# Between the stages of a vision layer with routed experts: tails, first weights and shared pieces in another order

## The reference

```python
    h = _L0_tok_ref(x, L0_tok_W, ...)
    h = h + _L0_attn_ref(_layernorm(h, axis=-1), L0_attn_W_c)
    h = h + _L0_ffn_ref(_layernorm(h, axis=-1), ...)
```

```python
        h = layer_norm(x, ln_in_g, ln_in_b)
        gate = jax.nn.softmax((h @ router_w + router_b) / TEMP, axis=-1)
        vals, idx = jax.lax.top_k(gate, TOP_K)
        ...
        eh = jax.nn.silu(jnp.einsum('bsd,edh->ebsh', h, ew1) + eb1[:, None, None, :])
        ey = jnp.einsum('ebsh,ehd->ebsd', eh, ew2) + eb2[:, None, None, :]
        mix = jnp.einsum('bse,ebsd->bsd', comb, ey)
        shared = (jax.nn.silu(h @ sw1 + sb1) @ sw2 + sb2) * SHARED_SCALE
        moe_out = mix + shared
        fh = layer_norm(moe_out, ff_ln_g, ff_ln_b)
        ff_out = jax.nn.silu(fh @ ff_w1 + ff_b1) @ ff_w2 + ff_b2
        return x + moe_out + ff_out
```

## Time and profile before

| | us |
|---|---|
| median of three runs | 976.31 |
| the three runs | 982.05, 968.53, 976.31 |
| span of the profiled execution | 972.0 |

### The profile page before, as it was taken

The page is one execution under the profiler, slowest core; times in us unless marked ns, Lnnn a source line. Parts: engine busy times, 40 slices in busy tenths (PEclk is TensorE's granted clock), DMA queues, the critical chain, the costliest instruction groups (busy, mean ns, idle before and its releaser), DMA issues. The chain is left out here.

```text
span 972.0 us, 22164 instructions
## 1 busy us (share of the span) xinstructions
PE 896.2 (92%) x5920; PEld 801.2 (82%) x5920; DVE 676.2 (70%) x2244; ACT 599.5 (62%) x1064; POOL 438.8 (45%) x374
## 2 busy tenths in 40 slices
PE   2999999989999999999889999999999899789999
PEld 2788888778878888888779889898999899679888
DVE  8377877757877887787556666666676675488884
ACT  3567666656666666777645565555555565477766
POOL 6012554425555545554451445455555464334342
PEclk9999999979999999999879999999999999989999
DMA  9999999977788888767137687777778675334432
GB/s 225 224 221 225 242 247 240 237 205 210 213 228 218 214 216 219 194 216 213 50 105 215 196 227 218 214 219 228 216 224 236 184 221 166 107 82 115 107 103 57
DMA packets 194299, 186.96 MB, mean 192 GB/s; under 512 B 16797, under 2 KB 168698, under 8 KB 194010
## 3 DMA queue, kind: packets, MB, share of 16 engines
q1 hardware_dynamic: 183168, 166.24, 65.2%
q0 software_dynamic: 9376, 19.42, 6.1%
q10 hardware_dynamic: 1722, 0.93, 0.5%
HBM read 150.48 MB, written 36.04 MB: 192 GB/s over the span
## 5 line engine op out<-in xcount | busy, mean ns | idle before, releaser
L1435 PE MATMUL bank<-xf,wp 128*128 128x256 f32 x1280 | 314.0, 394 | 8.4 <-ACT xf L632 5.4
L1435 PEld LDWEIGHTS bank<-xf,wp 128*128 128x128 f32 x1280 | 237.7, 192 | 51.6 <-issue 7.4
L916 POOL DMA_INDIRECT y_tok<-region,dsti x160 | 162.9, 1018 | 164.9 <-DVE region L1268 119.0
L874 POOL TENSOR_TENSOR rstd<-var,neghalf 128x4 f32<-128x4 f32 (+2 forms) x51 | 80.6, 1580 | 287.9 <-DVE var L1030 156.4
L632 ACT ACTIVATE xf<-region 128x1024 f32<-128x1024 f32 x160 | 174.0, 1137 | 18.3 <-DVE region L947 18.3
L890 POOL DMA_INDIRECT z_rows<-z,posg x130 | 157.3, 1210 | 52.5 <-issue 52.2
L798 ACT ACTIVATE region<-bank,cols 128x256 f32<-128x256 f32 x320 | 132.3, 476 | 55.2 <-PE bank L1626 37.2
L1637 PE MATMUL bank<-region 128*128 128x128 f32 x1280 | 156.8, 275 | 1.1 <-DVE region L1268 1.0
L1637 PEld LDWEIGHTS bank<-region 128*128 128x128 f32 x1280 | 150.4, 192 | 1.7 <-issue 1.5
L1626 PE MATMUL bank<-parts 128*128 128x256 f32 x960 | 136.6, 290 | 14.2 <-DVE parts L1279 8.8
L1626 PEld LDWEIGHTS bank<-parts 128*128 128x128 f32 x960 | 119.6, 190 | 25.7 <-issue 19.0
(11 more groups left out here) (183 smaller groups left out, 1232.3 us busy)
## 6 DMA issues: line engine op xcount, KB each, us to landing
region<-in_x SPq DMA_DIRECT2D x384, 196.0 KB
region<-in_L_ffn_ew SPq DMA_DIRECT2D x160, 256.0 KB
region<-z_rows SPq DMA_DIRECT2D x80, 130.0 KB
region<-y_tok SPq DMA_DIRECT2D x16, 512.0 KB, 3.6
ht_dram<-hT SPq DMA_DIRECT2D x16, 256.0 KB
r_dram<-rr SPq DMA_DIRECT2D x16, 256.0 KB
region<-ht_dram SPq DMA_DIRECT2D x16, 256.0 KB, 5.5
region<-r_dram SPq DMA_DIRECT2D x16, 256.0 KB
```

Of the source, the lines that this page charges most:

```text
L874: pool.tensor_tensor(dst, var, neghalf[:, 0:var.shape[1]], ALU.pow).then_inc(ready, 1)
L916: pool.indirect_dma_start(y_tok, bass.IndirectOffsetOnAxis(dsti[n % 2][:, i:i + 1], 0), yout[n % 2][:, i], None).then_inc(y_free[n % 2], 16)
L1435: ins = pe.matmul(out_cols, wp[:, s], cols_in, start=s == 0, stop=s == MAIN - 1)
```

## The change

Four parts:

- SP zeroes the tails 4 to 11 before it waits for the scatters, not after it has loaded the rows of the tiles 0 to 3.
- SP loads w1 of tile 4 before its loops, and within them w1 of tile j + 1 between the rows and w2 of tile j. `four_loads` replaces the four calls of `expert_loads`; it loads the expert number of its first tile once more. The last four tiles are written out behind the second loop, which has one pass less.
- Pieces of the shared expert change places: on TensorE `sh_up(7)` goes ahead of the last group's transposes, and three pieces go ahead of the table's transposes; on ScalarE and VectorE the matching steps move with them.
- VectorE splits w1 of tile 0 before it waits for the table's transposes.

```diff
-            def expert_weights(j, n):
-                ex = sp.value_load(ejc[0:1, bass.ds(j, 1)], min_val=0, max_val=E - 1)
+            def expert(j):
+                return sp.value_load(ejc[0:1, bass.ds(j, 1)], min_val=0, max_val=E - 1)
+
+            def first_weight(j, n, ex):
                 sp.wait_ge(w1l_ready, j - 3)
                 sp.dma_start(w1b[n % 4], ew1[bass.ds(ex, 1)].rearrange("o d h -> d (o h)")).then_inc(w1_loaded[n % 4], 16)
+
+            def second_weight(j, n, ex):
                 sp.wait_ge(down_done, j - 3)
...
-            def expert_loads(j, n):
-
-                expert_rows(j, n)
-                expert_weights(j, n)
-
+            def four_loads(j, n, end=4):
+
+                ex = expert(j)
+                for m in range(4):
+                    expert_rows(j + m, n + m)
+                    if m < end:
+                        coming = expert(j + (m + 1))
+                        first_weight(j + (m + 1), n + m + 1, coming)
+                    second_weight(j + m, n + m, ex)
+                    ex = coming
+
+            zero_tails(sp, FIRST, SP_TAILS)
             sp.wait_ge(tails_first, 16 * FIRST)
             sp.wait_ge(z_free[0], 16 + 16 * TOPK + 16 * TOPK * GT * GROUPS // 2)
             sp.wait_ge(z_free[1], 16 + 16 * TOPK * GT * GROUPS // 2)
             for j in range(FIRST):
                 sp.dma_start(zin[j], z_rows[j * CAP:j * CAP + EROWS].rearrange("(p h) d -> p h d", p=P))\
                   .then_inc(zin_loaded[j], 16)
-            zero_tails(sp, FIRST, SP_TAILS)
+            sp.wait_ge(w1l_ready, 1)
+            sp.dma_start(w1b[0], ew1[FIRST]).then_inc(w1_loaded[0], 16)
...
-                for n in range(4):
-                    expert_loads(i * 4 + n, 4 + n)
+                four_loads(i * 4, 4)
             sp.dma_start(r_res[:, PATCH_TILES * D:], r_dram[:, PATCH_TILES]).then_inc(r_loaded, 16)
-            with sp.Fori(1 + GROUPS, EXPERT_TILES // 4) as i:
-                for n in range(4):
-                    expert_loads(i * 4 + n, 4 + n)
+            with sp.Fori(1 + GROUPS, EXPERT_TILES // 4 - 1) as i:
+                four_loads(i * 4, 4)
+            four_loads(EXPERT_TILES - 4, EXPERT_TILES - 4, end=3)
...
+            sh_silu(FILL)
             one(take_z, GROUPS)
-            shared(FILL)
+            ht_high(FILL + 2)
...
                 if not attn:
                     ht_low(FILL)
+                    sh_rows(4)
...
                 if not attn:
-                    sh_rows(4)
                     ht_low(FILL + 1)
+                    sh_rows(5)
...
             dve.tensor_copy(tail[:, :], base[0:1, :]).then_inc(tail_ready, 1)
+            ht_low(FILL + 2)
+            sh_rows(FILL - 1)
...
-            sh_rows(FILL - 2)
+            ht_low(FILL + 3)
+            split_w1(0, 0, 0)
             dve.wait_ge(tej_done, 1)
...
+            sh_up(FILL)
             t_zz(GROUPS, 0)
-            sh_up(FILL)
             gates(GROUPS, 0)
```

More of the change, by code:

```diff
@@ L1250, in _ @@
             dve.wait_ge(tab_ready, 1)
-            split_w1(0, 0, 0)
-            for i in range(FILL, EARLY):
+            sh_rows(FILL)
+            for i in range(FILL + 2, EARLY):
                 if i + 2 < EARLY:
@@ L1596, in _ @@
             sh_up(FILL + 1)
+            sh_down(FILL)
+            sh_up(FILL + 2)
+            sh_down(FILL + 1)
             pe.wait_ge(ejt_ready, 1)
@@ L1602, in _ @@
             pe.matmul(bank[7][:, 0:DYN], ones[:, :], ejd[:, :], start=True, stop=True).then_inc(ejb_done, 1)
-            for i in range(FILL + 2, EARLY):
-                sh_down(i - 2)
+            for i in range(FILL + 3, EARLY):
                 sh_up(i)
-            sh_down(EARLY - 2)
+                sh_down(i - 1)
             sh_down(EARLY - 1)
```

## The result

The changed kernel takes 996.73 us (median of six runs, 990.79 to 999.93) against 975.58 for the kernel before (six runs, 968.53 to 982.05): a ratio of 1.0219, 95% interval 1.018 to 1.0258. It is slower by 2.2%, 21 us, where I forecast 6 us slower. The sign was right; the time lies 0.7 us outside the range that I gave.

A forecast was written before the change was run, and what follows sets the result against it. SP, issuing without a pause, was taken to bound the second stage. Earlier start -6.0, extra load in seventeen passes +13.6 and end -1.4 gave +6.2 us on the median 976.31, put at 982; range 966 to 996.

The forecast's parts named there:

- SP sets the second stage: Expert tiles: SP, issuing without a pause, takes 15.68 us a pass where the PE alone needs 13.72.
- What would show it: List of signs for right or wrong, such as SP hardly waiting, a pass of 16.3 to 16.7 us, zin waits grown.
- The stretch of 15.68 over the clean 14.1: Expert loop: measured pass over one of four clean tiles plus 1.5 us; raised a load's price from 0.74 to 0.8 us.
- Asking for w1 a tile ahead removes none of SP's work: Expert loop: the earlier request leaves SP's work as it was; only the extra expert-number load was charged, 0.8 us a pass.
- Term (c): Expert loop until tile 76: seventeen passes with one more register load each, +13.6 us.
- Tails, 6.98 us hidden: Before the expert loop: eight tails on SP move inside its 8.3 us wait for the scatters, taking 6.98 us off.
- Shared pieces, -1.1 and -2.63 on the PE: Before the first expert tile: moved pieces bring the gates 1.1 us earlier and fill 2.63 us of PE idling.
- waits that were there: Before the expert loop: moved pieces on VectorE and ScalarE fall into existing waits, with no cost counted.
- the forecast 6 us earlier start of tile 8: Start of the expert loop: SP's zin load of tile 8 comes at 534.6 instead of 540.66, 6.0 us earlier.
- Term (d): Behind tile 76, where only the PE runs on: 20.2 us instead of 21.55 with w1 early, 1.4 us off.
- The whole stage speeds up: Rival, expert loop: SP's slow steps come from VectorE's lateness and vanish; -21.7 us, or 955; chance 0.06.
- hidden load: Rival, expert loop: the extra load disappears in waits the profile doesn't name; -8.2 us, or 968; chance 0.22.

The follow-up runs named there:

- e9: The kernel before, with SP's register loads stripped of the test of their bounds: ratio 1.0108 (1.0017 to 1.0199).
- e10: The kernel before, with a tile's row and expert numbers loaded together from one table, without the bounds test: ratio 1.0005 (0.997 to 1.004).
- e5: The kernel before, with GpSimd storing results to plain consecutive rows by direct DMAs instead of scatters: ratio 0.9695 (0.9582 to 0.9809).
- e6: The changed kernel, with GpSimd storing results to plain consecutive rows by direct DMAs instead of scatters: ratio 0.9682 (0.9558 to 0.9806).
- e4: The kernel before, with w1 asked for a tile ahead only inside a pass, still four expert numbers loaded: ratio 1.0162 (1.0106 to 1.0218).
- e14: The changed kernel, with GpSimd's second scatter of a tile held until the PE's second product of the next tile: ratio 1.0119 (1.0041 to 1.0197).
- e3: The kernel before, with one unused register load of an expert number added to each pass: ratio 1.0118 (1.0034 to 1.0202).
- e1: The changed kernel with the loop of before, leaving the moved shared pieces and tails: ratio 0.999 (0.9945 to 1.0034).
- e12: The changed kernel with the loop of before and the tails in their old place, leaving the moved pieces: ratio 0.999 (0.9954 to 1.0027).
- e7: The kernel before, with a pass's eight register loads made as two loads of four values at its start: ratio 1.045 (1.0339 to 1.0561).

## Why the prediction was wrong, point by point

- *SP sets the second stage.* Half right. SP still has hardly a wait in the changed kernel, the wait for w1 went and that for zin came, as written under "What would show it". But SP's pace was not made of its own work alone: an estimated 2 to 3.6 us a pass taken off it gained nothing (e9, e10), and taking the result scatters away gave the PE's pace (e5, e6). The stretch of 15.68 over the clean 14.1, which I put into the load's price as a factor, was the scatters.
- *The failed step: "Asking for w1 a tile ahead removes none of SP's work", with no cost set for it.* It adds no work, and yet it costs about 16 us (e4). The runs show where: in the changed kernel SP's steps beside scatters take 1.63 us more a pass (steps of the added load among them), and without scatters the cost is gone (e5, e6). How the order brings SP and scatters together is argued from the traces: the PE now pauses for zin, 29 times, more than half of that time at a pass's first tile and never at its fourth; results then come more often two tiles together, and fours go from 5 to 17. Pacing the scatters took 6 to 10 of the 21 us back (e14), not all that the order costs.
- *Term (c), the extra load, 13.6 us.* If anything too large: 11.5 us by e3's ratio (3 to 20), 7 by its pass, 4 without its one long run. The Trainium skill's 200 ns for a register load ("Runtime: NRT & Kernel Launch", section "Instruction fetch mechanics"), some 4 us here by an estimate from that page, lies at the low edge of that; the 0.74 us of the earlier trace rows speaks against it, and e3 does not settle it. What failed was to take the pass as it was plus one load: it grew by 1.71, not 0.8.
- *Tails, 6.98 us hidden.* The prediction named what could take the cover away, SP's slow steps beside the scatters, allowed 3 us and counted none. In e1 at least 5.8 us of it were gone, and the first tiles' rows came 7.4 us after the last scatter instead of 1.5.
- *Shared pieces, -1.1 and -2.63 on the PE.* The idle time moved instead of going: 5.64 us for ScalarE in the changed kernel, 6.10 for VectorE in e12, both behind PE signals that came late. The prediction put the moved pieces on VectorE and ScalarE into "waits that were there", and counted nothing for a longer one. Together with the tails, the forecast 6 us earlier start of tile 8 became 2.3 us later, seen from the last scatter.
- *Term (d), -1.4.* Measured -0.6.
- *The rivals.* "The whole stage speeds up" (955) and "hidden load" (968) are out as forecasts of the time. "Slower: a slow load" forecast 1003 and a pass of 1.88 us more; the time comes near, but its mechanism falls with e3 and e4.

Still open is what in the chip lets a scatter delay SP's instructions and the PE's signals: the runs show when it happens and what it costs, not by what way. Also open is why the order brings the scatters into fours in some passes and not in all, and what the rest of the order's cost is that stays when they are paced.

## What to carry to other kernels

An engine without waits need not be the bound: look at the length of its steps and at what else runs beside the long ones, then take that away in an experiment before charging work against a pace. In this kernel the scatters on GpSimd slowed SP's instructions and the PE's signals while they ran, so look for the same where a stage scatters: count them as a cost of the whole stage, try them further apart, and do not count on hiding work beside them. Asking for data earlier can cost time even where it adds no work, as e4 did; the traces suggest that it pulled evenly spread work into bunches.

## What the runs showed of the hardware

- Beside GpSimd's indirect DMAs, most of them 0.96 to 1.2 us long, SP took about 0.7 us for single steps that in e5 have a median of 0.06 to 0.41 us by their kind, and ScalarE's instruction started up to 4.6 us behind the modelled end of the PE's products (0.9 at most in e5). With direct DMAs of the same size from GpSimd, about 1.15 us for two, e5 and e6 show hardly any of this in the second stage (1 and 3 such steps).
- On SP the step from one batch of four tails to the next, with the register loads of four row numbers, took 1.96 us behind the scatters (before) and 6.5, most of it beside them, in e1.
- In the seven traces with the moved pieces VectorE waited 4.97 to 6.58 us for the table that the PE had transposed, until 0.2 to 1.8 us behind the last scatter; in the ten others at most 0.15 us.
- Fewer instructions on SP made the kernel slower where they bunched the work: 4.5% with one load of four values in place of four loads (e7).
